# Turned biases, TensorE dummies, the order of the expert list and fp32 shared down products in a two-layer hybrid block

## What is computed

```python
x = x + attn_a(layernorm(x))   # 32 heads of 64, state 128, causal conv, gated; a scan over tokens
x = x + ffn(layernorm(x))      # ffn adds its own input: n + shared + routed
x = x + attn_b(layernorm(x))   # 64 heads of 8, state 128, gated
x = x + ffn(layernorm(x))

# ffn on n = layernorm(x); 16 routed experts, 2 of them per token; 2 shared experts, on every token
aff = sigmoid(n @ wa)
p, i = top_k(aff, 2); p = p / sum(p)
expert(n) = (gelu(n @ g + gb) * (n @ w1 + b1)) @ w2 + b2      # 256 -> 128 -> 256
ffn(n) = n + sum_shared expert(n) + sum_k p_k * expert_{i_k}(n)
```

## Time and profile before

| | us |
|---|---|
| median of 3 runs | 1099.77 |
| the runs | 1099.74, 1099.77, 1107.16 |
| the profiled execution | 1107.84 |
| its span, first to last instruction | 1106.5 |

### The profile page before, as it was taken

How to read it: one execution, slowest core, us unless ns; L and a number is a source line. 1 busy time by engine, 2 the same in 40 slices (tenths; PEclk the granted TensorE clock), 3 DMA queues, 4 the chain that set the end, 5 groups by cost and what they waited for, 6 DMA issues and landing times.

```text
span 1106.5 us, 22666 instructions
## 1 busy us (share of the span) xinstructions
PE 943.3 (85%) x9110; PEld 736.3 (67%) x9110; DVE 711.6 (64%) x1247; ACT 583.3 (53%) x920; POOL 663.2 (60%) x670
## 2 busy tenths in 40 slices
PE   7810399999999999999999996999588886988993
PEld 6600387888888888888888875666466355865661
DVE  5700488888878889787888665432595966354433
ACT  5800488776868777687776350122387444140221
POOL 4600756887867788686786845576238723224772
PEclk9965699999999999999999996799699989995996
DMA  3661321211112212121110571232512115041233
GB/s 109 30 1 5 117 66 68 68 49 68 62 46 66 77 39 77 50 69 57 39 49 2 165 209 36 69 84 47 180 39 63 22 32 150 24 133 53 84 87 116
DMA packets 67092, 77.64 MB, mean 70 GB/s; under 512 B 17139, under 2 KB 55123, under 8 KB 66983
## 3 DMA queue, kind: packets, MB, share of 16 engines
q1 hardware_dynamic: 61037, 63.85, 22.0%
q0 software_dynamic: 5952, 12.34, 4.1%
HBM read 63.65 MB, written 12.55 MB: 69 GB/s over the span
## 4 chain that ended last, share of the span: by engine, by line
PE 59%; DVE 19%; POOL 6%; SPq 5%; DMA 4%; issue 4%; ACT 3%; DVEq 0%; POOLq 0%; ACTq 0%
PE psum L784 20%; PE psum L1079 7%; DVE arena L1907 6%; PE psum L756 4%; PE psum L863 4%; PE psum L1098 4%; SPq L565 4%; PE psum L855 3%; PE psum L908 3%; DVE arena L1944 2%; DMA scratch_a<-arena 2%; SPq L594 1%; PE psum L1066 1%; PE psum L1209 1%; PE psum L1076 1%
## 5 line engine op out<-in xcount | busy, mean ns | idle before, releaser
L784 PE MATMUL psum<-vT,split 128*128 128x512 f32 x1368 | 348.1, 404 | 6.2 <-DVE arena L1907 5.0
L1907 DVE SCALAR_TENSOR_TENSOR arena<-psum,arena 128x1023 f32<-128x1023 f32 (+2 forms) x208 | 265.9, 1278 | 81.1 <-ACT arena L1402 57.5
L784 PEld LDWEIGHTS psum<-vT,split 128*128 128x128 f32 x1368 | 250.0, 189 | 65.6 <-DVE arena L1907 7.1
L1402 ACT ACTIVATE arena<-psum,arena 128x512 f32<-128x512 f32 x160 | 109.2, 690 | 73.9 <-PE psum L784 73.0
L863 PE MATMUL psum<-arena 128*64 128x64 f32 x1792 | 62.5, 225 | 69.1 <-POOL arena L2504 69.1
L863 PEld LDWEIGHTS psum<-arena 128*64 128x64 f32 x1792 | 57.6, 140 | 74.7 <-issue 74.6
L2469 POOL TENSOR_TENSOR split<-arena,split 128x256 fp32r<-128x256 f32 x114 | 83.6, 741 | 33.3 <-ACT split L1327 33.3
L1419 ACT ACTIVATE arena<-arena 128x1024 f32<-128x1024 f32 x80 | 84.4, 1058 | 33.8 <-POOL arena L2496 22.8
L2496 POOL TENSOR_TENSOR arena<-arena,v 128x1021 f32<-128x1021 f32 x32 | 76.3, 2386 | 42.7 <-DVE arena L1907 42.7
L2487 POOL TENSOR_TENSOR bcast<-bcast,arena 128x1024 f32<-128x1024 f32 x32 | 60.8, 1900 | 68.0 <-DMA bcast<-scratch_a 68.0
L2695 POOL DMA_INDIRECT bcast<-scratch_v,arena x62 | 60.6, 978 | 38.4 <-PE psum L1066 13.2
(11 more groups left out here) (275 smaller groups left out, 1804.3 us busy)
## 6 DMA issues: line engine op xcount, KB each, us to landing
bcast<-scratch_a SPq DMA_DIRECT2D x32, 512.0 KB, 3.6
arena<-in_w_a SPq DMA_DIRECT2D x16, 768.0 KB, 4.2
arena<-scratch_y SPq DMA_DIRECT2D x16, 256.0 KB, 4.3
arena<-in_wout_a SPq DMA_DIRECT2D x8, 256.0 KB, 2.6
scratch_v<-v SPq DMA_DIRECT2D x8, 256.0 KB
arena<-in_wg SPq DMA_DIRECT2D x4, 512.0 KB, 5.5
arena<-in_wu SPq DMA_DIRECT2D x4, 512.0 KB, 6.4
arena<-in_wd SPq DMA_DIRECT2D x2, 1024.0 KB, 9.1
```

The lines of the kernel that those rows point to most:

```text
L784: m = pe.matmul(bank, split[:, t % SPLITS, i, q, :], vT[:, j, q, half * BANK:(half + 1) * BANK], start=(n == 0), stop=(n == 3 * KD - 1))
L1402: act.activation(tile[:, hs], wide_of(t)[:, hs], ACT.Identity, scale=w[:, TAPS - 1:TAPS], bias=0.0).then_inc(sem["tap0"], 1)
L1907: dve.scalar_tensor_tensor(out=tile[:, s:T], in0=bank[:, 0:T - s], scalar=cw_a[:, j, i, TAPS - 1 - s:TAPS - s], in1=tile[:, s:T], op0=ALU. ...
```

## The change

**Biases.** The turned transfers and `scratch_r` go. b2 is loaded into 18 partitions of a buffer in the accumulator `A["acc"]`; a new unit "bias" in FILLED holds two transposes of gb and ub, made by TensorE before pair 0, and ACT copies it beside b2. The three bf16 parts are made in pairs 0 and 1 (ACT `bias_part`, GpSimd `bias_rest`), SP writes them at pair 2 and waits for the landing, and the first output product of the layer waits for that too, since it overwrites the buffer.

```diff
-                for at, name in ((0, "gb"), (F, "ub")):
-                    sp.dma_start(scratch_r[:, at:at + F], io[name].rearrange("f e -> e f"),
-                                 allow_slow_non_contiguous=True).then_inc(sem["braw"], 16)
-                load("braw", scratch_r[:, 2 * F:BIASES], io["b2"])
+                load("b2", raw_bias[:, 2 * F:BIASES], io["b2"])
...
+                    if j == 2:
+                        on.wait_ge(sem["bias_p"], 4)
+                        load("bias_s", scratch_p.rearrange("i e n -> e i n"), parts_e)
+                        on.wait_ge(sem["bias_s"], 16)
...
+                on.wait_ge(sem["gb"], 16)
+                on.wait_ge(sem["ub"], 16)
+                bank = open_bank("bias")
+                for i, columns in enumerate((gb, ub)):
+                    m = pe.transpose(bank[0:EXPERTS, i * F:(i + 1) * F], columns[:, :], ident[:, :])
+                m.then_inc(sem["unit"], 1)
...
+                act.copy(raw_bias[:, 0:2 * F], bank_of("bias")[0:EXPERTS, 0:2 * F]).then_inc(sem["act_done"], 1)
                 for j in range(PAIRS):
                     nxt = j + 1
+                    if j < 2:
+                        bias_part(j)
...
                     carry_u(j, 1)
                     first_zero(j)
+                    if j < 2:
+                        bias_rest(j)
```

```diff
                     for c in range(4 * half, 4 * half + 4):
-                        for m_, (iw, ih) in enumerate(PRODUCTS):
-                            m = pe.matmul(out_cols(c), split_hid[:, s % 2, ih, (c % 4) * P:(c % 4 + 1) * P],
-                                          split_down[:, p % DOWNS, iw], start=(p == 0 and c % 2 == 0 and m_ == 0),
-                                          stop=False, skip_group_check=True)
+                        m = pe.matmul(out_cols(c), hid_e[:, s % 2, (c % 4) * P:(c % 4 + 1) * P],
+                                      w_e[:, p, 2 * KD * F:WORDS], start=(p == 0 and c % 2 == 0), stop=False,
+                                      skip_group_check=True)
```

```diff
                 down(0)
+                rank()
                 up(3)
                 down(1)
-                rank()
+                keep_busy(out_cols(6), BUSY_LIST)
+                members()
                 down(2)
-                members()
                 down(3)
+                turn_in(0)
                 shared_bias()
-                turn_in(0)
                 turn_in(1)
...
                 hidden(0)
                 route_first()
+                route_second()
                 hidden(1)
-                route_second()
+                places()
                 hidden(2)
-                places()
+                tokens()
+                results()
                 hidden(3)
-                last_lo()
-                tokens()
                 owners()
-                results()
                 shares()
```

```diff
-BUSY_NORM = ((12, 4, 4, 0), (5, 5, 5, 0), (16, 5, 5, 0), (5, 5, 5, 0))
+BUSY_NORM = ((12, 4, 4, 0), (5, 5, 5, 0), (45, 5, 5, 0), (5, 5, 5, 0))
+BUSY_LIST = 10
...
+                for r in range(RING):
+                    on.wait_ge(sem[f"sct{r}"], 16 * n_given(n, BLOCKS - 1, r))
+                for q in range(NC // 2):
+                    act.dma_start(y_e[:, 1, 2 * q:2 * q + 2, :], result_rows(1, q)).then_inc(sem[f"yl{q}"], 16)
```

More of the change, by code:

```diff
@@ L319 @@
 DECAY_ACT = {"a": ["alog", "eexp", "ln", "elo", "eneg", "ehi", "wd", "dec"], "b": ["alog", "eexp", "ln", "inv"]}
-ROUTER = ["inc", "recip", "max1", "eq1", "key1", "km1", "one1", "aff2", "max2", "eq2", "key2", "km2", "one2", "mask"]
+ROUTER = ["inc", "max1", "eq1", "key1", "km1", "one1", "aff2", "max2", "eq2", "key2", "km2", "one2", "mask"]
 ROUTER += ["up", "count", "by1", "by2", "by4", "ends", "starts", "place", "picked", "slot", "high", "base", "mark", "row", "hot0", "hot1"]
-ROUTER += ["second", "token", "before", "nth", "capped", "at_w", "at_b", "nobody", "result", "sum", "share", "parts"]
+ROUTER += ["second", "token", "nobody", "result", "before", "nth", "capped", "at_w", "at_b", "each", "sum", "share", "parts"]
 FIELDS = ("dt", "t1", "hi", "cumlo", "tothi", "totlo", "t0", "t2", "t3", "lo", "cumhi", "wd", "dec")
@@ L2180, in shares @@
                 def shares():
+                    dve.reciprocal(G_["best"], G_["best"]).then_inc(sem["router"], 1)
+                    after("each")
                     dve.tensor_tensor(G_["den"], best[:, 0], best[:, 1], ALU.add).then_inc(sem["router"], 1)
```

130 lines of the change are left out of this document (39 added, 91 removed).

## The result

| | us |
|---|---|
| before, 4 runs (median) | 1099.74, 1099.77, 1102.92, 1107.16 (1101.35) |
| after, 4 runs (median) | 1004.41, 1004.66, 1005.74, 1009.03 (1005.2) |
| after : before | 0.9125, 95% interval 0.9082 to 0.9168 |
| profiled execution, before and after | 1107.84 and 1004.41 |
| its span, before and after | 1106.5 and 1003.0 |

Much faster, as forecast, but the time lies 13 us under the forecast of 1018 and 7 us under the range. Between the two profiled executions it is 103.4 us, where the terms added up to 89.5.

The account below looks back on a forecast made before the run. It took TensorE's 69.08 us wait in the first layer, then the expert lists, as the bound. From 1107.84 us, 65 + 5.1 + 7.8 + 5.1 + 5.0 + 0.8 + 0.7 = 89.5 gave 1018; range 1012 to 1026, with rivals to 1036.

Parts of the forecast that it names:

- The stop of 69 us: First layer, first state products: TensorE's 69.08 us wait was whole-kernel time, caused by decay rows queued behind the turned loads.
- The term of 65: First layer: replacing the turned bias transfers saves a net 65 us (62 to 67), with state products starting near 62.
- The restart at full clock: First state products: 56 records that took 3.09 us at low clock would run at full clock, saving 1.3 us.
- The rival in which the row write was slow by itself: First layer: the decay-row write's 19.87 us are its own, so 48.6 us saved for 65.1, total 1034; chance 0.05.
- The list: Expert list, both layers: earlier ranks (3.8 us) and a shorter way to the tokens (1.3) start block 0 5.1 us sooner.
- the rival in which the clock still falls: Lists: costs the blocks' 7.8 or 5.0 us plus 1.8 in down steps; 1025 to 1028, or 1034 both; chance 0.33.
- fp32 products: Shared down products: a step takes 1.77 us for 1.60, while ACT's and GpSimd's splits disappear off the path.
- Dummies and clock: Lists: 20 dummy records keep the clock full, so first blocks start 2.44 us apart, gaining 7.8 and 5.0 us.
- GpSimd as the bound of the blocks: Expert blocks: GpSimd needs 2.59 us a block against TensorE's 2.44, costing 7.5 us, total 1026; chance 0.08.
- the 0.8 us: Layer tail: 90 dummy records for 32 keep first transposes and normalization at full clock, gaining 0.8 us (0 to 2).
- The final term, 0.7: Final additions: ACT's queue issues half of the final loads, gaining 0.7 us (0 to 1.2).
- The 8 us above the median: The profiled execution of before exceeds the median by 8 us, read as one more half-clock stretch; the forecast does not fall by it.

Follow-up runs that it names:

- the experiment: The kernel after with all 16 final loads of an expert layer issued by SP, none by ACT; ratio to before 0.9133 (0.9103 to 0.9163).
- place 116 to 118: Recorded TensorE instructions before L1221, modulo 256: kernel after twice, after with final loads on SP, before with 48 tail dummies; stretch 46.3, 48.9, 46.7, 47.3 us.

## Why the prediction was right in direction and too low in size

The step that failed is that the sum priced the second layer at nothing: the layer became 7.4 us shorter, half of the 14 us by which the sum of 89.5 fell short of 103.4. The rest are sizes: the first layer 69.0 us for 65, the blocks 15.8 for 12.8, the lists 11.3 for 10.2; the two tails gave 0.1 for 1.5. Their mechanisms hold in the main, but not everywhere.

**The stop of 69 us** was read rightly, and the removal did what was said. The term of 65 was 4 us short. The landing was taken as 3.4 us from a larger write and is 2.1; the issue stood at 39.92, not 41.3; the row load took 4.3 us, not 5.8. So the first row came at 46.3, not 50.5, before GpSimd was free, at 47.26, and the states began at 59.12, not 62.3. The restart at full clock brought 1.2 us in the first records, as the term had it. The 1.2 us of GpSimd's subtraction don't show: it starts at 59.08, behind the steps for the first states, and has cover. The waits of SP for the biases cost nothing: from the second eighth of the state products to the last, each eighth starts 69.1 or 69.2 us sooner than before. The rival in which the row write was slow by itself is out: the same write landed in 2.1 us without the element transfers in front of it. One reading was off: of the two long issues only the one of 15.20 us is a turned load; that of 34.61 is b2, plain rows that stood behind the turned ones.

**The list** gave 6.9 and 4.4 us to block 0, forecast 5.1 each. Ranks start right behind the first down step, at 593.27, as said, which gained 4.0 us on that step (forecast 3.8); from the ranks to the tokens it is 2.2 us less (forecast 1.3), and from the tokens to block 0 another 0.7. (The mask's end comes to 662.3 by the earlier trace rows, not 661.3; that is still ahead of the ranks.) In experts(1) the tokens gained 5.4 us on the first down step, and the clock took 1 us of it back: the two last down steps took 5.38 us, at half clock for 3.4 us. So of the rival in which the clock still falls a part came true in this layer: the 1.8 us that it had for the down steps, not the 5.0 of the blocks. By the other profiles such a fall comes in some executions and not in others: the repeat of the kernel after has none.

**fp32 products.** The size of a step was about right: 1.89 us for 1.77 forecast, against 1.60. The estimate of 2.13 us, made from the four passes of the Trainium skill ("FP8 and Floating Point Precision", TensorE Precision Notes), was too high; it took each pass at the 0.133 us of a fp32r record, while a quarter of a fp32 product of 256 columns is 0.11 us in the earlier trace rows, so the price of a pass was off, and nothing here speaks against four of them. Wrong is that the splits "disappear off the path": they stand on it. With them put back the last down steps waited 2.34 us for GpSimd and ran mostly at half clock, and a layer was 3.4 us longer.

**Dummies and clock.** The forecast of full clock in the first blocks held, in both layers. Its reason did not: the 20 records in the list matter for the down steps alone, 0 to 2.65 us in single pairs of profiles and some 1.7 a layer on average, while the blocks ran at full clock without them too. The gain in the blocks was 9.4 and 6.4 us, forecast 7.8 and 5.0. That size was off by my counting: a window of 22.4 us was set against six times 2.44, but it ended before the sixth slow interval did, and at full clock the first two intervals are 2.11. The first six intervals took 23.35 us before and 13.97 after, 9.4 less; the first four of experts(1) 15.01 and 9.09, 5.9 less. GpSimd as the bound of the blocks is out: intervals stayed at 2.44 to the end.

**Tails.** The first transposes at full clock are there (0.93 us for 1.18), but they stand 0.3 us further from the last scatter (11.38 us for 11.05). The second queue is not the reason, since with all loads on SP it is 11.46; the cause is open, and the 0.8 us are about nothing. The final term, 0.7, measured 0.4 between the first two profiles, 0.8 in the experiment and 0.7 between the means of all.

**What the sum had not at all:** the second layer, 7.4 us. The waits of TensorE listed 9.7 us without a semaphore at one line before the change; I had not asked what they were, and so took that layer as the same. They stand at the seams of TensorE's blocks of 256 instructions, and a shift of the program moves these seams to other products. Executions of one kernel differ there too, by up to 6 us before, but the mean of this layer (transposes to third up step) over five profiles of before is 195.7 us, over four at place 116 to 118 it is 189.0, so most of the 7 us belongs to the kernel. In the stretch measured above about half of it is idle time; the rest is clock, and why the clock falls less in the kernel after is not shown.

**The 8 us above the median.** The prediction said that the sum against the slow profile "does not come down by these 8 us", since they were a half-clock stretch that the change removes. That step is shaky: most of what one faster execution of before gained stands in the second layer, where nothing was meant to change. The spread did shrink: on the faster chips the executions of before lie between 1095.5 and 1108.7 us, the ten of after between 1003.7 and 1009.0. What makes a stretch of before vary from run to run is open.

## What to carry to other kernels

A transfer that moves single elements costs more than its place in the queue: while it ran here, rows, writes and even instruction packets came late, so turn small tables on TensorE. Look for stops without a semaphore in long runs of tiny matmuls before calling a stage unchanged; count the instructions ahead of each, modulo 256, and if they agree, the stops move with every instruction that you add or take away in front, and some us appear or vanish in a stage that nobody edited. Dummies are worth what stands right behind the idle time they fill; price them by an experiment without them, and by more than one pair of profiles, since the clock falls in some executions of a kernel and not in others.

## What the hardware showed unexpectedly

- All 73 stops of TensorE in that stretch of the second layer, in 17 profiles, stand behind the same count of recorded instructions modulo 256 (193) and end 1.2 to 1.6 us behind the end of a 16 KB instruction packet; the packets came no closer than 3.3 us there, each for some 256 instructions.
- Under the transfers by elements an instruction packet took 7.5 us for about 1, and two engines stood 9 to 11 us without a semaphore.
- The granted clock falls in a list in some executions of a kernel and not in others: with dummies in 5 of 14 lists, without them in 4 of 4.
- The size of a second-layer stretch went with the clock as much as with stops: 37.9, 40.1 and 43.2 us for the same products at a mean clock of 1.00, 0.93 and 0.87.
- Chips differ: the kernel before took 1101 us (medians) on two and 1133 to 1141 on two others, while up to the ranks of experts(0) the same program differed by 3.7 and 6.0 us. The ratio after : before (or its nearest kin) stayed at 0.911 to 0.917.
